# Another order of the opening with identity matmuls, and binary products as 64x64 tiles fed by six transfers in place of twelve

## What is computed

```python
h = _L0_tok_ref(x, ...)                       # attention in 8x8 windows, 8 heads, rotary encoding
h = h + _L0_attn_ref(_layernorm(h), ...)      # attention to the 7x7 neighbourhood
h = h + _L0_ffn_ref(_layernorm(h), ...)       # two hidden layers with a routed expert
h = h + _L1_attn_ref(_layernorm(h), ...)      # attention with decay 0.99 and no softmax
h = h + _L1_ffn_ref(_layernorm(h), ...)       # the binary layer
```

```python
gate = (sigmoid(x @ proj_w.T + proj_b) > 0.5)       # 8 gates of 0 or 1
w = einsum('e,eio->io', gate, weight)               # a 64x64 matrix of the token's own
y = sign(x) @ sign(w)                               # then y * scale
```

## Time and profile before

| | |
|---|---|
| median of 3 runs | 1708.08 us (1706.97 to 1711.36) |
| profiled execution, its own time | 1710.65 us |
| its span, first to last instruction | 1708.8 us |
| PE / PEld busy | 1568.4 us (92%) / 1169.1 us (68%) |
| DVE / ACT / POOL busy | 1212.2 us (71%) / 1041.2 us (61%) / 613.4 us (36%) |
| mean granted TensorE clock | 0.967 of full speed |

### The profile page before, as it was taken

One profiled execution on the slowest core, in us unless ns is written; L12 is line 12 of the kernel. 1 busy time (PEld: TensorE's weight loads), 2 busy tenths in 40 slices (PEclk: granted clock), 3 DMA queues, 4 the chain that ended last, 5 costly groups with the idle time before them and its releaser, 6 DMA issues.

```text
span 1708.8 us, 83280 instructions
## 1 busy us (share of the span) xinstructions
PE 1568.4 (92%) x29546; PEld 1169.1 (68%) x29546; DVE 1212.2 (71%) x3605; ACT 1041.2 (61%) x2053; POOL 613.4 (36%) x923
## 2 busy tenths in 40 slices
PE   5899999779999999999986899999999999999996
PEld 3677777657777777777764667667667667667663
DVE  1566666547888878788755778778778778778762
ACT  2565655444444444444421578878878878878876
POOL 3242222166666666666622212212212212212210
PEclk9999999869999999999995899999999999999997
DMA  3201001034444444444420233333333333333332
GB/s 105 79 25 31 25 30 31 12 103 117 126 123 121 121 120 127 124 122 122 123 74 22 66 84 83 88 83 83 88 83 83 88 83 83 88 83 83 88 77 56
DMA packets 134833, 143.15 MB, mean 84 GB/s; under 512 B 42770, under 2 KB 90258, under 8 KB 134514
## 3 DMA queue, kind: packets, MB, share of 16 engines
q1 hardware_dynamic: 126450, 116.07, 26.0%
q10 hardware_dynamic: 8320, 26.22, 5.7%
HBM read 66.42 MB, written 16.99 MB: 49 GB/s over the span
## 4 chain that ended last, share of the span: by engine, by line
PE 66%; issue 8%; DVE 8%; DMA 5%; ACT 4%; SPq 4%; POOL 2%; ACTq 1%; DVEq 1%; POOLq 0%
PE ps_D L901 12%; DVE prob L1469 4%; PE ps_D L811 4%; PE ps_D L687 4%; DMA k_d<-kpad 3%; PE ps_AV L918 3%; PE ps_OT L830 3%; SPq L465 2%; PE ps_J L1009 2%; PE ps_J L977 2%; PE ps_AV L838 2%; PE ps_J L959 2%; PE ps_OT L653 2%; PE ps_J L1040 2%; PE ps_AV L697 2%
## 5 line engine op out<-in xcount | busy, mean ns | idle before, releaser
L1211 ACT ACTIVATE prob<-ps_D 128x1024 bf16<-128x1024 f32 x448 | 459.4, 1029 | 121.2 <-PE ps_D L901 119.3
L1181 ACT ACTIVATE prob<-ps_D 100x512 f32<-100x512 f32 x256 | 139.0, 595 | 166.2 <-PE ps_D L811 166.2
L811 PE MATMUL ps_D<-tile_a,key_patch 64*100 64x128 f32 x2048 | 175.9, 289 | 0.0
L560 POOL TENSOR_TENSOR tile_a<-q_st,q_mask 128x512 f32<-128x512 f32 x128 | 135.2, 1056 | 112.5 <-PE ps_D L811 93.5
L901 PE MATMUL ps_D<-tile_a,w_parts 128*128 128x256 bf16 x1024 | 153.9, 276 | 11.0 <-DVE xg L1506 3.0
L901 PE MATMUL ps_D<-tile_b,w_parts 128*128 128x256 bf16 x1024 | 152.5, 274 | 12.4 <-DVE xg L1506 3.4
L807 PE MATMUL ps_D<-mT,key_rows 64*100 64x128 bf16 x1024 | 124.4, 226 | 25.1 <-ACT prob L1181 25.1
L534 POOL TENSOR_TENSOR rstd_bin<-veps_bin,minus_half 128x2 f32<-128x2 f32 x64 | 44.2, 691 | 269.4 <-DVE veps_bin L1272 269.4
L1373 DVE TENSOR_REDUCE m_sb<-ps_D 128x4 f32<-128x400 f32 x256 | 134.5, 566 | 8.9 <-PE ps_D L788 8.5
L811 PEld LDWEIGHTS ps_D<-tile_a,key_patch 64*100 64x100 f32 x2048 | 140.3, 167 | 0.0
L534 POOL TENSOR_TENSOR rstd_ret<-veps_ret,minus_half 128x2 f32<-128x2 f32 x64 | 46.6, 728 | 247.7 <-DVE veps_ret L1272 247.7
(11 more groups left out here) (179 smaller groups left out, 4010.6 us busy)
## 6 DMA issues: line engine op xcount, KB each, us to landing
tile_a<-xg SPq DMA_DIRECT2D x384, 64.0 KB, 2.0
tile_b<-xg SPq DMA_DIRECT2D x384, 64.0 KB, 2.0
key_st<-k_d SPq DMA_DIRECT2D x128, 162.0 KB, 3.0
tile_b<-v_d ACTq DMA_DIRECT2D x128, 120.0 KB
tile_b<-v_d ACTq DMA_DIRECT2D x64, 160.0 KB
w_exp<-experts SPq DMA_DIRECT2D x64, 129.0 KB, 2.3
xT<-in_x SPq DMA_DIRECT2D x32, 256.0 KB, 2.6
k_d<-kpad SPq DMA_DIRECT2D x64, 64.0 KB, 2.9
```

The costliest lines, as they stand in the source:

```text
L560: gp.tensor_tensor(q_block[:, par, :].rearrange("c (p h q) -> c p h q", h=NH, q=NQ)[:, own, :, :], q_st[:, par, :].rearrange("c (p a q) -> ...
L811: mm = pe.matmul(s_loc[x][0:NKL, u * P:(u + 1) * P], key_patch[rows_of(x), par, at * NKL:(at + 1) * NKL], q_block[rows_of(x), par, at * P: ...
L1181: act.activation(prob1[0:NKL, 2 * g + x, :], s_loc[x][0:NKL, :], ACT.Exp).then_inc(T2["exp_done"], 1)
L1211: act.activation(sgn[:, k % 4, :], unit(k, par)[:, :], ACT.Sign).then_inc(BN["sign"], 1)
```

## The change

```diff
@@ SP: spread_in
-                for part in range(3):
-                    for n in range(4):
-                        sp.dma_start(x_parts[par][32 * part:32 * (part + 1), 1024 * n:1024 * (n + 1)], xg[32 * n:32 * (n + 1), :]).then_inc(BN["x_in"], 16)
+                for half in range(2):
+                    for part in range(3):
+                        at = C * half + 16 * part
+                        sp.dma_start(x_parts[par][at:at + 16, :], xg[rows_of(half), :]).then_inc(BN["x_in%d" % par], 16)
@@ SP: ahead of loop three
+            sp.wait_ge(s_clear, 4)
             staggered(sp, strips)
@@ POOL: ahead of loop three
-            gp.memset(tile_a[PARTS:P, :, :], 0.0).then_inc(s_clear, 1)
-            gp.wait_ge(s_clear, 1)
-            gp.memset(tile_b[PARTS:P, :, :], 0.0).then_inc(s_clear, 1)
-            gp.wait_ge(s_clear, 2)
+            for n, (tile, at) in enumerate(((tile_a, 32), (tile_a, 96), (tile_b, 32), (tile_b, 96))):
+                if n:
+                    gp.wait_ge(s_clear, n)
+                gp.memset(tile[at:at + 32, :, :], 0.0).then_inc(s_clear, 1)
+            gp.wait_ge(s_clear, 4)
@@ PE: opening
+            def keep_busy(n):
+                for _ in range(n):
+                    pe.matmul(s_tok[0][:, 0:P], ident[:, :], ident[:, :], start=True, stop=True)
+            pe.wait_ge(s_const, 1)
+            for _ in range(3):
+                pe.matmul(s_tok[0][:, :], tile_b[:, 0, 0:P], tile_b[:, 0, 0:512], start=True, stop=True)
             pe.wait_ge(s_w, 16 * NFIRST)
...
             tok_project(NT - 2)
+            keep_busy(6)
             tok_project(NT - 1)
+            keep_busy(18)
             pe.wait_ge(s_later, 16 * NLATER)
@@ PE: front of loop two
                     pre_turn(m, 0)
+                    keep_busy(2)
                     pre_values(m, m % 2)
                     pre_keys(m, m % 2, 0)
+                keep_busy(10)
@@ PE: weights
-                        for a in range(2):
-                            at = (2 * (k % 2) + a) * 4 + k // 2
-                            mm = pe.matmul(d[:, a * 512 + oh * 256:a * 512 + (oh + 1) * 256], w_parts[:, at, oh, :, :].rearrange("r i o -> r (i o)"),
-                                           x_parts[half][:, at * 256:(at + 1) * 256], start=True, stop=True)
+                        for lanes in range(2):
+                            for x in range(2):
+                                at = 2 * k + lanes
+                                mm = pe.matmul(d[rows_of(lanes), x * 512 + oh * 256:x * 512 + (oh + 1) * 256],
+                                               w_parts[rows_of(x), at, oh, :, :].rearrange("r i o -> r (i o)"),
+                                               x_parts[half][rows_of(x), at * 256:(at + 1) * 256], start=True, stop=True)
@@ PE: the matmul on ysum, now once for each x and half of the tokens
-                        mm = pe.matmul(bank["T"][:, 256 + t * C:256 + (t + 1) * C], ysum[:, t * P:(t + 1) * P], half_sum[:, :], start=True, stop=True)
+                        for x in range(2):
+                            mm = pe.matmul(bank["T"][:, 256 + t * C:256 + (t + 1) * C], ysum[:, 256 * x + t * P:256 * x + (t + 1) * P], half_sum[:, :],
+                                           start=x == 0, stop=x == 1)
@@ DVE: gate_weights
-                if j in (3, 4):
-                    for lane in (2 * j - 6, 2 * j - 5):
-                        dve.tensor_scalar(w_parts[0:PARTS, :, :, lane, :], w_sel.rearrange("p (n h o) -> p n h o", n=16, h=2),
-                                          lane_mask[0:PARTS, lane:lane + 1], None, ALU.mult).then_inc(s_placed, 1)
+                if j in (2, 3, 4):
+                    for lane in range(2):
+                        dve.wait_ge(s_placed, 7 + 2 * (j - 2) + lane)
...
+                        if j == 2:
+                            dve.tensor_scalar(dst, src, own, None, ALU.mult).then_inc(s_placed, 1)
+                        else:
+                            dve.scalar_tensor_tensor(out=dst, in0=src, scalar=own, in1=dst, op0=ALU.mult, op1=ALU.add).then_inc(s_placed, 1)
```

More of the change, by code:

```diff
@@ L243, in build @@
         RT = named("ret", "stats", "mv", "veps", "rstd", "xn", "xT_ps", "xT_sb", "uv_ps", "ud", "v", "kd", "s_ps", "sd", "state", "out_ps", "h_done")
-        BN = named("bin", "stats", "mv", "veps", "rstd", "xn", "xs", "g_ps", "gates", "x_ps", "xg", "x_in", "w_ps", "sign", "clip",
+        BN = named("bin", "stats", "mv", "veps", "rstd", "xn", "xs", "g_ps", "gates", "x_ps", "xg", "x_in0", "x_in1", "w_ps", "sign", "clip",
                    "y_part", "ysum", "y_ps", "ys", "y", "stored")
@@ L738, in _ @@
             tok_qk(0, 0, 0)
+            keep_busy(16)
             tok_keys(0, 0)
             tok_v(0, 0)
+            tok_qk(1, 0, 1)
             tok_max(0, 0, 0)
             tok_max(0, 0, 1)
-            tok_qk(1, 0, 1)
+            for _ in range(9):
+                pe.matmul(bank["AV"][:, 0:P], ident[:, :], ident[:, :], start=True, stop=True)
             pairs(pe, tok)
             tok_project(NT - 2)
+            keep_busy(6)
             tok_project(NT - 1)
+            keep_busy(18)
             pe.wait_ge(s_later, 16 * NLATER)
@@ L916, in reduce @@
                     for k in (2 * pair, 2 * pair + 1):
-                        for cg in range(4):
-                            mm = pe.matmul(bank["AV"][32 * cg:32 * (cg + 1), 0:256], lane_sum[:, int(k == 1), :], sgn[:, k % 4, cg * 256:(cg + 1) * 256],
-                                           start=k == 0, stop=k == 7)
+                        for oh in range(2):
+                            cg = 2 * (k % 2) + oh
+                            mm = pe.matmul(bank["AV"][32 * cg:32 * (cg + 1), :].rearrange("o (x t) -> o x t", x=2), lane_sum[:, int(k == 1), :],
+                                           sgn[:, k % 4, :].rearrange("r (x h t) -> r h x t", x=2, h=2)[:, oh, :, :], start=k < 2, stop=k >= 6)
                     mm.then_inc(BN["y_part"], 1)
@@ L949, in strips @@
                     weights(3, par, unit(3, par))
+                    pe.wait_ge(BN["ysum"], times(q))
+                    reduce(q, 0)
                 if f is not None or g is not None:
@@ L961, in strips @@
                         pe.matmul(bank["T"][:, 0:256], w_gate[C:P, :], xfgT[C:P, :], start=True, stop=True).then_inc(BN["g_ps"], 1)
-                if q is not None:
-                    pe.wait_ge(BN["ysum"], times(q))
-                    reduce(q, 0)
                 if r is not None:
@@ L1217, in strips @@
                     act.wait_ge(BN["y_ps"], times(p))
-                    act.activation(ysum[:, :], bank["AV"][:, 0:256], ACT.Copy).then_inc(BN["ysum"], 1)
+                    act.activation(ysum[:, :], bank["AV"][:, :], ACT.Copy).then_inc(BN["ysum"], 1)
                 if f is not None or g is not None:
```

48 lines of the change are left out of this document (24 added, 24 removed).

## The result

The changed kernel runs in 1695.85 us (median of 4, 1694.73 to 1698.65), the kernel before in 1708.46 beside it: a ratio of 0.9924 (95% interval 0.9906 to 0.9941), 12.6 us faster where 28 were predicted. Direction and places were as forecast, the size was not: the time lies inside the 1660 to 1698 of the likeliest case and the 1640 to 1712 of the range, but the gain is less than half.

A forecast was written before the change was run, and what follows sets the result against it. The prediction took PE's matmuls to bound the steady strips and xg's copies the loop's end. Strips -16, tail -7, start of loop three +5, opening -6.5 and front -3 sum to -27.5, about 1680 us, range 1640 to 1712.

The forecast's parts named there:

- A unit, 0.34: Loop three's products: eight 256-column matmuls in four tiles take 0.34 us, where four matmuls took 0.44.
- Step (a): Strip from unit 3 to hid, with the sum now ahead of it: 1.22 becomes 1.29 us, +0.07.
- Steps (b), (c) and unit 5: Unit 4 with the exit from tiles behind it +0.10, four small ysum matmuls for two +0.06, unit 5 -0.10 us.
- Step (d): Units 5, 6 and 7 of the strip: -0.10 us each, -0.30 together.
- Step (e): Units 0 and 1 ahead of the clip: -0.20 us; leaving tiles after unit 7 charged nothing, 0.20 if uncovered.
- Six transfers in the tail: Loop three's end: six xg issues fewer a strip save about 3.4 us in each of two strips, -7; steady strips hide them.
- Start of loop three: Two more POOL clears and slower weight placing on DVE, less earlier first transfers: +5 us.
- Opening: Loop one's start: new order -3 us, earlier full PE clock through filler matmuls -3.5, together -6.5.
- `front`: End of loop one and start of loop two: filler matmuls raise PE's clock over three turns, -3 us.
- the first (a unit near 0.22): Rival: tiles give nearly all, a unit takes 0.22 to 0.28 us, whole time 1610 to 1650; chance 0.19.
- the third (tiles take turns): Rival: tiles above each other don't overlap, a unit takes about 0.5 us, whole time 1720 to 1770; chance 0.12.
- The second (changes of mode eat the gain): Rival: each of four returns to whole-array matmuls costs 0.20 us, the strip stands still, 1696 to 1712; chance 0.14.

The follow-up runs named there:

- red_back: Changed kernel with the first sum over the signs back behind the two matmuls on xfgT, as before the change: 1688.74 us.
- best3: Changed kernel with two clears over all rows, SP's wait moved to the first xg transfer, and first sum moved back with unit 4 beside it: 1675.82 us.
- one_tile: Changed kernel plus one unread 64-column matmul a strip in a 64 x 64 tile, between L1035 and the spread: 1718.60 us.
- before_eight: Kernel before with eight xg transfers a strip instead of twelve (weights' low parts left out, output wrong) and clears over all rows: 1699.76 us.
- issues12: Changed kernel with six small copies a strip issued behind the six xg transfers, so twelve issues again: 1705.60 us.
- two_clears: Changed kernel with POOL clearing each tile in one instruction over 128 rows instead of two over 32 rows: 1689.67 us.
- fill_open: Changed kernel with only the opening's unread matmuls, without those at the end of loop one and in front: 1695.21 us.
- best4: best3 without the unread matmuls around the end of loop one and in loop two's front: 1672.00 us.
- halves: Changed kernel issuing only the four matmuls of each unit on the upper 64 rows (output wrong): 1697.59 us.
- u0_early: Changed kernel with the next strip's unit 0 ahead of the state's four matmuls instead of behind them: 1703.74 us.
- one_full: Changed kernel plus one unread 64-column matmul a strip on the whole array, in the same place as in one_tile: 1706.09 us.

## Why the prediction missed

The step that failed is the walk of the strip: -0.27 us was predicted and -0.085 measured. The mean distances between PE's groups over 38 strips (start to start, us), by the names of the changed kernel, tell the strip apart piece by piece:

| from, to | in between | before | after | red_back | best3 |
|---|---|---|---|---|---|
| L966, L986 | units 2, 3; after: first sum | 1.77 | 1.98 | 1.86 | 1.86 |
| L986, L1001 | before, red_back: first sum; best3: and unit 4 | 1.35 | 1.33 | 1.32 | 1.67 |
| L1001, L1011 | unit 4 (not best3) | 0.94 | 0.94 | 0.94 | 0.54 |
| L1011, L1035 | unit 5, a sum, `ysum` | 1.75 | 1.81 | 1.81 | 1.70 |
| L1035, L1066 | unit 6, a sum | 2.67 | 2.58 | 2.58 | 2.58 |
| L1066, L1077 | unit 7 | 0.93 | 0.93 | 0.93 | 0.93 |
| L1077, L966 | units 0, 1, a sum | 2.23 | 1.99 | 1.99 | 1.99 |

- **A unit, 0.34**: right to the hundredth for units 4 to 7; units 2 and 3, each right behind a wait, take 0.41 on the chain. **The pair behind unit 4, 0.63**: right.
- **Step (a), the sum moved (+0.07)**: the first that failed. I wrote "there PE waits for `hid` anyway". It did not: before, the sum was the work that filled that wait. Moved ahead, it lengthens the first row (+0.21, with units 2 and 3 in it), and the second stays (1.35 to 1.33), since PE now stands idle for the 0.26 us of the view of waits. Rows one and two together are +0.19 where +0.07 was predicted; `red_back` takes 0.13 back. Even then they are +0.06, though units 2 and 3 are 0.1 shorter each: I had not seen that PE waits for sign 0 there. The step also set 0.34 against the 0.60 of unit 3, a unit behind a wait, which is 0.41 now.
- **Steps (b), (c) and unit 5 (+0.06 in sum)**: rows three and four, +0.06.
- **Step (d), unit 7 (-0.10)**: row six, 0. The exit behind it, which I charged at nothing in (e) since sign 7 would cover it, is paid on PE's own chain (0.37 for the first L1077 pair, 0.17 for L1051 before). Unit 6, next to its sum, gained its 0.09. So a unit that stands alone between whole-array matmuls pays for its tiles at least what they save, 0.10; `one_tile` (0.19) and `best3` (0.16) show the price from both sides.
- **Step (e), units 0 and 1 (-0.20)**: row seven, -0.24. The chain, which does not run through L966, splits rows six and seven otherwise: unit 7 gains its 0.10, the exit behind it costs the 0.20 that I had charged at nothing, and from unit 0 to unit 3 it is 2.11 for 2.46, since the way leads through sign 0 (1.03) and unit 2 instead of the clip (1.24). The exit, in the chain of before, beside 1212.98 above:

```profile
1218.25 0.17 PE ps_OT L1051 x2
```

- The strip: -0.27 + 0.12 (a) + 0.10 (d) - 0.04 (e) = -0.09, measured -0.085. Over 60 strips that is 11 of the 16 us between forecast and median; `front` is 3 more.
- **Six transfers in the tail (-7)**: -6.6 from the 57th clip to the last. The step was right, its working half so. The issues fell from 7.5 to 3.8, but landing grew: in the chain the last transfer of the ring takes 4.98 and 5.13 us in place of 1.98 to 2.95, and the last two distances between `xg` are 10.35 and 10.78, not 9. That they are "hidden behind PE" in the steady strips is true of before (`before_eight`). It is also what lets the tiles gain there: with six small issues more they gain nothing (`issues12`, 11.666).

```profile
1653.66 4.98 DMA tile_b<-xg
...
1658.77 1.24 DVE xg L1533
...
1675.06 5.13 DMA tile_b<-xg
```

- **Start of loop three (+5)**: +6.0 to the first clip, of which the two further clears are 2.4 to 3.6 (`two_clears`). Then 1.9 us come back in the next eight strips, 0.7 of it the strip's own gain; the rest fits the ring of before, which was in the way there (its strip from the fourth to the fifth clip took 12.56 us, 11.65 in `before_eight`).
- **Opening (-6.5)**: -8.0. The order (-3) gave 2.4 in the traces, as predicted; the fillers' clock (-3.5) gave 5.6 and was sized too small. The keys' pair of tile 1 takes 0.67 and not the predicted 0.43; at the full clock of before it took 0.43 once and 0.63 the next time.
- **`front` (-3)**: -0.3, and neither `fill_open` nor `best4` loses time without the bundles. Loop two starts 9.7 us earlier (345.3, 335.6) and is 8.1 earlier at the values of strip 9 (403.9, 395.8), so in this pair the gain of the first turns isn't kept. The pair alone says little. From the last tile's queries to the values of strip 9 the 14 traces with bundles take 89.8 to 94.1 us, 92.7 on average, and the six without 91.6 to 98.0, 95.2 on average (92.7 in that of before). Some 2 us may thus be gained up to there; that they are missing from the whole times stays unexplained.

Of the rivals, the first (a unit near 0.22) and the third (tiles take turns) are refuted by the unit's 0.34 and by `halves`. The second (changes of mode eat the gain), with a chance of 0.14, came nearest: its 1696 to 1712 begins where 1695.85 was measured. The exit that isn't covered is half of the mechanism; it lacked the other half, the sum's place, which `red_back` shows to cost 0.13. What stays open: how the wait for sign 0 is to be covered, which `u0_early` failed to do, and what the bundles behind the opening do.

## What to carry to other kernels

Before moving work out of a place, ask what wait it fills there: a piece of work in front of a dependent matmul can be free where it stands and cost its full length elsewhere. Tiles on PE paid a fixed price for each stretch of them here, so count stretches and not matmuls, and put tiled pieces side by side. With fewer transfers the ends of the loop gain what the middle hides; `before_eight` shows that this needs nothing of the tiles, though a kernel of before with six whole transfers wasn't run. And compare one place over several traces before a difference of a few us is given a cause.

## What the runs showed of the hardware

- Two tiles in other rows of the array cost nothing beside the first two: 0.34 us for a unit with four matmuls or with eight (`halves`, the change).
- A way into and out of tiles cost 0.19 us (`one_tile` less `one_full`), about half of it on either side. The fp32 pairs right behind tiles took 0.20 more than those behind whole-array work (0.63 for 0.43, 0.37 for 0.17).
- Three matmuls of 512 columns that nobody reads, ahead of the first product, went with a first product of 0.67 us in place of 1.19 and with the full clock some 30 us earlier. Whether the 25 short ones behind them are needed too wasn't tested.
- Transfers of 16 rows and 128 KB land 4.2 us after issue and those of 32 rows and 64 KB after 2.0 (page, DMA issues, before and after), for the same bytes a strip; the DMA share rises from 0.34 to 0.51. The reason wasn't tested.
- Splitting them to 8 rows took the strip from 11.56 to 15.35 us, with PE at a mean clock of 0.83 meanwhile.
- Clearing 128 rows of 2048 columns took POOL 1.80 us, as did 32 rows.
